# Row maxima of eight heads in one VectorE instruction over two PSUM banks

## The chip, the cores and the metric

The kernel runs on one core of a Trainium2 chip. The metric is device time in microseconds of one execution. The chip's engines, each with its own instruction queue: PE (TensorE, the matrix engine), VectorE (DVE in the rows), ScalarE (ACT), GpSimd (POOL) and SyncE (SP). They meet only at semaphores. PE writes its results to PSUM, which has eight banks of 512 float32 columns on 128 partitions; VectorE and ScalarE read them there.

## The reference

The input is x, 16 sequences of 128 tokens with 128 features. A first layer is a transformer block with conditioning: normalisation, attention with 16 heads of 8 features (q and k normalised and rotated), projection, then a gated feed-forward. A second layer is a linear attention. The change touches the softmax of the first layer only:

```python
attn = jnp.einsum('bnhd,bmhd->bhnm', q, k) * scale
attn = jax.nn.softmax(attn, axis=-1)
o = jnp.einsum('bhnm,bmhd->bnhd', attn, v).reshape(B, N, C)
```

For each sequence and each head this needs the maximum over 128 keys for each of 128 queries, so that the exponential is taken of scores less their maximum.

## The kernel before

All work is scheduled by hand. Each engine has a function `step(t, p)` that holds its share of several sequences at different stages; `steps` runs it for t from −5 to 16. Steps 3 to 10 are a hardware loop with two steps a pass, the others are written out. In step t the scores and their row maxima belong to sequence t + 1, the softmax and the values to sequence t, the splitting of q and k into bf16 parts ("cut", L1282 to L1291) to sequence t + 2, the square sums of q and k ("seed", L1301 to L1311) to sequence t + 4, and the output to sequence t − 1. Within an engine the order is that of the code; `wait` and `wait_ge` hold an engine until a semaphore has reached a value.

The scores of a sequence are made twice. The first time PE writes them as q·k into two banks in turn, `S_BANK` = (0, 1), four heads (512 columns) a bank, in four chunks: `scores(0)` to `scores(3)` (L1468). VectorE takes the row maxima of each chunk with `rowmax(c)` (L1268), negated, into `nmax`. When all 16 are there, VectorE casts them to bf16 in two parts (L1358, L1363), PE transposes them (L1507), and in the next step `weighted(c)` (L1453, L1454) computes scores less maxima in the banks 2 and 3, from which ScalarE takes the exponential (L1062) into `probs`. `values` (L1480) multiplies by v.

`stack(half)` (L1498) is eight PE transposes of q and k parts into bank 4. `stack(0)` serves sequence t + 2, and VectorE copies it to `qT` and `kT` (L1348 to L1350); `stack(1)` is the other half, copied by ScalarE.

What orders the work around the row maxima:
- `scores(c)` overwrites the bank that `rowmax(c − 2)` has read, so it waits for that maximum (`s_max`, raised once by each `rowmax`).
- `rowmax(c)` waits for `scores(c)` (`s_s`).
- In a step PE's order is stack(1), scores(0), transposes (L1507, L1512, L1517), weighted(0), weighted(1), scores(1), L1526, L1530, weighted(2), scores(2), stack(0), projection (L1537), weighted(3), scores(3), values, L1547.
- VectorE's order is cut(0), the padding of v (L1319), L1325, cut(1), L1331, rowmax(0), cut(2), rowmax(1), rowmax(2), the copies of the stack bank, rowmax(3), seed(0) (L1301), the cast L1358, seed(1) (L1305), L1363, L1367, seed(2) (L1307), seed(3) (L1311), L1374.
- GpSimd takes the result of seed(3) through a Newton iteration (L998 to L1004), scales the rotated q and k (L1007), and prepares the next sequence (L965 to L993).

After the attention the same banks 0 and 1 serve the feed-forward (`GU_BANK`), whose first matmul waits for the last row maximum.

Of the kernel before, what the change touches and what calls it, by code (L numbers as in the profile page):

```python
# [26 lines left out]
F32 = mybir.dt.float32  # L27
# [5 lines left out]
B, T, D = 16, 128, 128  # L33
# [14 lines left out]
HPC = 4  # L48
NC = H // HPC
# [23 lines left out]
def is_seq(b):  # L73

    return not isinstance(b, int) or 0 <= b < B


def wait(eng, sem, value):

    if not isinstance(value, int) or value > 0:  # L80
        eng.wait_ge(sem, value)
# [44 lines left out]
def dit_then_linear_attention(nc, x, cond, pos, norm1_w, qkv_w, q_norm_w, k_norm_w, proj_w, proj_b,  # L126
                              norm2_w, w1, w3, w2, ada_w, ada_b, norm_g, norm_b, Wq, bq, Wk, bk, Wv,
                              bv, emb_W, emb_b, sn_g, sn_b, out_W, out_b, out):
    ctx = ExitStack()
    with ctx:  # L130
# [76 lines left out]
        nmax = [sb(f"nmax{p}", [128, H]) for p in range(2)]  # L207
# [44 lines left out]
        hg = two("hg", UNIT, T)  # L252
        res = sb("res", [128, B, D])

        bank = [ctx.enter_context(nc.psum_tensor(f"bank{i}", [128, 512], F32)) for i in range(8)]
        S_BANK, E_BANK, STACK_BANK, P_BANK, O_BANK, W_BANK = (0, 1), (2, 3), 4, 5, 6, 7
        GU_BANK, F_BANK, FT_BANK, X_BANK = (0, 1, 4), 2, 3, 7

# [34 lines left out]
        s_s = sem("s_s")  # L293
        s_max = sem("s_max")
# [476 lines left out]
        def blocks_tensor(e, start=None):  # L771
            q = nc.tensor
# [6 lines left out]
            def b_step(t, p):  # L779
                def hidden(c):  # L780
                    u = t + 1
                    if is_unit(u):
                        if c == 0:
                            e.wait_ge(b_hT, u + 1)
                            if at(u, 0):
                                e.wait_ge(s_max, NC * B)
                                e.wait_ge(s_st1, B)
                        wait(e, b_ff, FC * (u - 1) + c + 1)
                        q.matmul(bank[GU_BANK[c]][:, 0:UNIT * T], w1T[:, c * 128:c * 128 + 128], flat(hT2[1 - p]), start=True, stop=True)  # L789
                        q.matmul(bank[GU_BANK[c]][:, UNIT * T:], w3T[:, c * 128:c * 128 + 128], flat(hT2[1 - p]), start=True,  # L790
                                 stop=True).then_inc(b_gu, 1)

                def back(c):
                    if is_unit(t):
                        e.wait_ge(b_ff, FC * t + c + 1)
                        if c == 0:
                            wait(e, b_fg, t)
                            if at(t, 0):
                                e.wait_ge(s_p, NC * B)
                        last = q.matmul(bank[F_BANK][:, 0:UNIT * T], w2T[:, c, :], ff[c][:, :], start=c == 0, stop=c == FC - 1)  # L800
                        if c == FC - 1:
                            last.then_inc(b_fm, 1)
                back(0)
                hidden(0)
                if is_unit(t + 2):
                    e.wait_ge(b_xs, t + 3)
                    wait(e, b_hT, t + 2)
                    turned(bank[X_BANK], lambda j: xs2[p][:, j, :], b_xsT)
                back(1)
                back(2)  # L810
                hidden(1)
                hidden(2)
                if is_unit(t):
                    e.wait_ge(b_fg, t + 1)
                    wait(e, b_x2, t)
                    turned(bank[FT_BANK], lambda j: fg[:, j, :], b_fgT)
# [340 lines left out]
        def _(v):  # L1157
            q = nc.vector
# [101 lines left out]
            def step(t, p):  # L1260
                q0, q1 = p, (p + 1) % 2
                def rowmax(c):
                    if is_seq(t + 1):
                        b = t + 1
                        v.wait_ge(s_s, NC * b + c + 1)
                        if c == 0:
                            wait(v, s_mp, b - 1)
                        q.tensor_reduce(nmax[q1][:, c * HPC:(c + 1) * HPC],  # L1268
                                        bank[S_BANK[c % 2]][:, :].rearrange("p (h t) -> p h t", t=T),
                                        X_AXIS, ALU.max, negate=True).then_inc(s_max, 1)  # L1270


                def cut(k):
                    b = t + 2
                    if not is_seq(b):
                        return
                    both = parts[q0][:, :, :, :].rearrange("p s h (k d) -> p (s h) k d", d=DH)
                    pq = parts[q0][:, 0, :, :].rearrange("p h (k d) -> p h k d", d=DH)
                    pk = parts[q0][:, 1, :, :].rearrange("p h (k d) -> p h k d", d=DH)
                    if k == 0:  # L1280
                        v.wait_ge(s_hi, b + 1)
                        q.tensor_tensor(rest[:, :, :], rot[q0][:, :, :], both[:, :, 2, :], ALU.subtract).then_inc(s_parts, 1)  # L1282
                    if k == 1:
                        v.wait_ge(s_parts, PARTS * b + 1)
                        q.tensor_copy(both[:, :, 5, :], rest[:, :, :]).then_inc(s_parts, 1)
                    if k == 2:
                        v.wait_ge(s_parts, PARTS * b + 2)
                        q.tensor_tensor(pq[:, :, 4, :], rest[:, 0:H, :], pq[:, :, 5, :], ALU.subtract).then_inc(s_parts, 1)
                        q.tensor_tensor(pk[:, :, 1, :], rest[:, H:, :], pk[:, :, 5, :], ALU.subtract).then_inc(s_parts, 1)
                        q.tensor_copy(pq[:, :, 3, :], pq[:, :, 5, :]).then_inc(s_parts, 1)  # L1290
                        q.tensor_copy(pk[:, :, 0, :], pk[:, :, 5, :]).then_inc(s_parts, 1)  # L1291


                def seed(k):
                    b = t + 4
                    if not is_seq(b):
                        return
                    if k == 0:
                        v.wait_ge(s_sq, b + 1)
                        wait(v, s_newton, NEWT * (b - 2) + NEWT)  # L1300
                        q.tensor_reduce(qv_ms[q0][:, :], qk2[q0][:, :, :], X_AXIS, ALU.add).then_inc(s_ss, 1)  # L1301
                    else:
                        v.wait_ge(s_ss, SEED * b + k)
                    if k == 1:
                        q.tensor_scalar(qv_s[q0][:, :], qv_ms[q0][:, :], 0.5 / DH, 0.5 * EPS0, ALU.mult, ALU.add).then_inc(s_ss, 1)  # L1305
                    if k == 2:
                        q.tensor_scalar(qv_ms[q0][:, :].bitcast(I32), qv_s[q0][:, :].bitcast(I32), 1, None,  # L1307
                                        ALU.logical_shift_right).then_inc(s_ss, 1)
                    if k == 3:
                        wait(v, s_rot, ROT * (b - 2) + ROT)  # L1310
                        q.tensor_scalar(qv_y[q0][:, :].bitcast(I32), qv_ms[q0][:, :].bitcast(I32), -1.0,  # L1311
                                        float(MAGIC - 2 ** 22), ALU.mult, ALU.add).then_inc(s_ss, 1)

                cut(0)
                if is_seq(t):
                    b = t
# [16 lines left out]
                if is_seq(t + 5) and before(t, POOL_NORMS):  # L1333
                    b = t + 5
                    wait(v, s_xsT, b - 1)
                    q.tensor_scalar(xs[q1][:, :], xin[:, bass.ds(b, 1), :].rearrange("p a f -> p (a f)"),  # L1336
                                    rstd_x[:, bass.ds(b, 1)], None, ALU.mult).then_inc(s_xs, 1)
                rowmax(0)
                cut(2)
                rowmax(1)  # L1340
                rowmax(2)
                if is_seq(t + 2):
                    b = t + 2
                    v.wait_ge(s_st, 2 * b + 1)
# [3 lines left out]
                    q.tensor_copy(qT[q0][:, js, :], sb_[:, 0, :, :])  # L1348
                    q.tensor_copy(kT[q0][0:64, js, 0, :], sb_[0:64, 1, :, :])
                    q.tensor_copy(kT[q0][64:128, js, 1, :], sb_[64:128, 1, :, :]).then_inc(s_st0, 1)  # L1350
                rowmax(3)
                seed(0)
                if is_seq(t + 1):

                    b = t + 1
                    v.wait_ge(s_max, NC * b + NC)
                    wait(v, s_mTp, b)
                    q.tensor_copy(mparts[:, 0:H], nmax[q1][:, :]).then_inc(s_mh, 1)  # L1358
                seed(1)
# [30 lines left out]
        def _(e):  # L1390
# [50 lines left out]
            def step(t, p):  # L1441
# [15 lines left out]
                def scores(c):  # L1457
                    if not is_seq(t + 1):
                        return
                    b = t + 1  # L1460
                    if c == 0:
                        e.wait_ge(s_st0, b + 1)
                    if c == NC // 2:
                        e.wait_ge(s_st1, b + 1)
                    wait(e, s_max, NC * b + c - 1)
                    for i in range(HPC // 2):
                        j = c * (HPC // 2) + i
                        last = q.matmul(bank[S_BANK[c % 2]][:, i * 2 * T:(i + 1) * 2 * T], qT[q1][:, j, :],  # L1468
                                        kT[q1][:, j, :, :].rearrange("p s t -> p (s t)"), start=True, stop=True)
                    last.then_inc(s_s, 1)  # L1470
# [118 lines left out]
```

## Time and profile before

| | |
|---|---|
| median of 3 runs | 277.7 us (276.43 to 277.9) |
| profiled execution, span from first to last instruction | 274.4 us |
| time of the profiled execution around its span | not on the page |
| PE busy | 214.6 us (78%) |
| VectorE busy | 220.0 us (80%) |
| ScalarE busy | 169.7 us (62%) |
| GpSimd busy | 158.6 us (58%) |
| row maxima (L1268) | 64 instructions, 42.6 us |

The shares are averages over the loading of weights (to about 40 us), the attention steps (to about 165 us) and the feed-forward and second layer. A row of the timeline has start and duration in us from the span's start; PE's records overlap since matmuls are pipelined. In brackets stands the idle time of the engine before the row and what ended it.

### The profile page before, as it was taken

How to read it: one execution, taken by the hardware profiler on the slowest of the kernel's cores; microseconds unless marked ns; L12 is line 12 of the kernel's file. 1: busy time of each engine (PE TensorE's matmuls, PEld its weight loads, DVE VectorE, ACT ScalarE, POOL GpSimd, SP SyncE). 2: the span in 40 equal slices, each digit the busy share in tenths (PEclk: the TensorE clock that was granted, in tenths of full speed). 3: DMA queues.
4: the chain of work that ended last, by engine and by line, in shares of the span. 5: the costliest groups of instructions: out<-in, count | busy, mean ns of one | idle time of the engine just before them, and what ended most of it. 6: DMA issues, size and time to landing. Idle time of an engine off the chain costs nothing. (4 is left out here: it accounts for less than half of the span.)

```text
span 274.4 us, 7061 instructions
## 1 busy us (share of the span) xinstructions
PE 214.6 (78%) x2028; PEld 162.0 (59%) x2028; DVE 220.0 (80%) x700; ACT 169.7 (62%) x437; POOL 158.6 (58%) x431
## 2 busy tenths in 40 slices
PE   3406196998999989889899999599994899756763
PEld 2403053777677767767677777488882588533531
DVE  7495979899999999999999962587888899946322
ACT  0526235789898989889898875324340377654661
POOL 6184778888888887778887500011207486785300
PEclk9999565699999999999999999979999799995555
DMA  7710000000000000000000000000000000000112
GB/s 147 207 36 0 2 0 0 4 2 0 4 4 4 0 0 0 0 0 0 0 4 0 2 2 1 1 4 0 0 0 0 0 4 1 2 0 0 39 38 76
DMA packets 9554, 4.01 MB, mean 15 GB/s; under 512 B 2669, under 2 KB 9530, under 8 KB 9530
## 3 DMA queue, kind: packets, MB, share of 16 engines
q1 hardware_dynamic: 4170, 2.18, 2.9%
q10 hardware_dynamic: 5360, 1.54, 2.4%
q8 instruction: 11, 0.18, 0.3%
q14 instruction: 13, 0.11, 0.1%
HBM read 2.67 MB, written 1.05 MB: 14 GB/s over the span
## 5 line engine op out<-in xcount | busy, mean ns | idle before, releaser
L1268 DVE TENSOR_REDUCE nmax<-bank 128x4 f32<-128x512 f32 x64 | 42.6, 682 | 2.5 <-PE bank L1468 2.0
L1062 ACT ACTIVATE probs<-bank 128x512 f32<-128x512 f32 x64 | 37.6, 603 | 4.4 <-PE bank L1454 4.3
L1453 PE MATMUL bank<-qT,kT 128*128 128x128 bf16 x256 | 34.6, 222 | 0.3
L1454 PE MATMUL bank<-mT,sel 128*128 128x128 bf16 x256 | 34.5, 222 | 0.0
L1453 PEld LDWEIGHTS bank<-qT,kT 128*128 128x128 bf16 x256 | 25.4, 100 | 4.0 <-ACT mT L1095 1.3
L1454 PEld LDWEIGHTS bank<-mT,sel 128*128 128x128 bf16 x256 | 25.5, 99 | 2.8 <-issue 2.5
L1468 PE MATMUL bank<-kT,qT 128*128 128x256 bf16 x128 | 25.4, 282 | 0.6 <-DVE nmax L1268 0.6
L430 POOL TENSOR_TENSOR xs<-x,rstd 128x256 f32<-128x256 f32 x8 | 4.8, 612 | 32.6 <-DVE rstd L396 19.0
L543 ACT ACTIVATE th<-bank 128x256 f32<-128x256 f32 x24 | 9.2, 384 | 21.0 <-PE bank L776 11.1
L1498 PE MATMUL bank<-identb,parts 128*128 128x128 bf16 x256 | 20.8, 228 | 1.5 <-DVE kT L1350 0.9
L1498 PEld LDWEIGHTS bank<-identb,parts 128*128 128x128 bf16 x256 | 17.5, 104 | 5.2 <-DVE parts L1291 2.5
L1088 ACT ACTIVATE parts<-rot 128x384 bf16<-128x384 f32 x32 | 16.4, 523 | 6.5 <-POOL rot L1007 6.4
L1530 PE MATMUL bank<-qkvT,hT 128*128 128x384 f32 x32 | 16.0, 588 | 4.0 <-ACT hT L1102 4.0
L1480 PE MATMUL bank<-probs,vpad 128*32 128x128 f32 x512 | 17.7, 277 | 0.0
L1512 PE MATMUL bank<-ident,xs 128*128 128x128 f32 x16 | 5.3, 332 | 15.7 <-DVE xs L1336 15.7
L998 POOL TENSOR_TENSOR qv_t<-qv_y 128x32 f32<-128x32 f32 x48 | 12.2, 254 | 7.7 <-DVE qv_y L1311 4.5
L1002 POOL TENSOR_TENSOR qv_t<-three_halves,qv_t 128x32 f32<-128x32 f32 x48 | 14.3, 299 | 3.8
L1000 POOL TENSOR_TENSOR qv_t<-qv_t,qv_s 128x32 f32<-128x32 f32 x48 | 14.2, 297 | 3.8
L876 PE MATMUL bank<-hs,outw 128*128 128x256 f32 x16 | 9.6, 705 | 7.5 <-DVE hs L764 7.5
L1480 PEld LDWEIGHTS bank<-probs,vpad 128*32 128x32 f32 x512 | 12.6, 109 | 4.2 <-issue 3.2
L776 PE MATMUL bank<-ident,xs 128*128 128x128 f32 x48 | 11.4, 327 | 4.5 <-POOL xs L430 4.5
L789 PE MATMUL bank<-hT,w1T 128*128 128x256 f32 x48 | 14.7, 390 | 0.0
(247 smaller groups left out, 683.0 us busy)
## 6 DMA issues: line engine op xcount, KB each, us to landing
out_dram<-res SPq DMA_DIRECT2D x4, 256.0 KB, 2.3
xin<-in_x_dram ACTq DMA_DIRECT2D x1, 768.0 KB, 8.3
ada_n<-in_L_cond_ada_w_dram ACTq DMA_DIRECT2D x1, 384.0 KB, 3.7
xin<-in_x_dram ACTq DMA_DIRECT2D x1, 256.0 KB, 4.1
w_n<-in_L_cond_w_dram SPq DMA_DIRECT2D x2, 128.0 KB
qkv_n<-in_L_cond_qkv_w_dram SPq DMA_DIRECT2D x1, 192.0 KB, 4.5
w_n<-in_L_cond_w_dram SPq DMA_DIRECT2D x1, 170.5 KB
emb_n<-in_L_cond_emb_W_dram SPq DMA_DIRECT2D x1, 128.0 KB
```

What stands on the lines that cost most here:

```text
L789: q.matmul(bank[GU_BANK[c]][:, 0:UNIT * T], w1T[:, c * 128:c * 128 + 128], flat(hT2[1 - p]), start=True, stop=True)
L1000: q.tensor_tensor(t_, t_, s_, ALU.mult).then_inc(s_newton, 1)
L1002: q.tensor_tensor(t_, three_halves[:, :], t_, ALU.subtract).then_inc(s_newton, 1)
L1062: q.activation(probs[c][:, :, :].rearrange("p h t -> p (h t)"), bank[E_BANK[c % 2]][:, :], ACT.Exp, scale=SCALE).then_inc(s_p, 1)
L1088: last = q.activation(slots, rot[q1][:, s * H:(s + 1) * H, :].unsqueeze(2).to_broadcast([128, H, 3, DH]), ACT.Copy)
L1268: q.tensor_reduce(nmax[q1][:, c * HPC:(c + 1) * HPC], bank[S_BANK[c % 2]][:, :].rearrange("p (h t) -> p h t", t=T), X_AXIS, ALU.max, negat ...
L1453: q.matmul(dst, kT[q0][:, h // 2, h % 2, :], qT[q0][:, h // 2, :], start=True, stop=False)
L1454: last = q.matmul(dst, sel[:, h, :], mT[q0][:, :], start=False, stop=True)
L1468: last = q.matmul(bank[S_BANK[c % 2]][:, i * 2 * T:(i + 1) * 2 * T], qT[q1][:, j, :], kT[q1][:, j, :, :].rearrange("p s t -> p (s t)"), st ...
L1480: last = q.matmul(bank[O_BANK][VW * i:VW * (i + 1), c * T:(c + 1) * T], vpad[q0][:, c * HPC + i, :], probs[c][:, i, :], start=True, stop=True)
L1498: last = q.transpose(bank[STACK_BANK][:, at:at + T // 2].bitcast(BF16), src[:, s, h:h + 2, :].rearrange("p h k -> p (h k)"), identb[:, :])
L1530: q.matmul(bank[W_BANK][:, 0:3 * D], hT[q0][:, :], qkvT[:, :], start=True, stop=True).then_inc(s_qkv, 1)
```

## The change

Banks 0 and 1 become one PSUM tensor of 1024 columns, `both_s`. `rowmax(c)` is called twice instead of four times and reads both banks: rowmax(0) the eight heads of scores(0) and scores(1), rowmax(1) those of scores(2) and scores(3). The semaphore `s_max` rises by two a sequence instead of four, and the waits follow: scores(0) and scores(1) wait for both maxima of the sequence before, scores(2) and scores(3) for rowmax(0) of their own. On VectorE cut(2) now stands ahead of rowmax(0), and seed(0) ahead of rowmax(1).

```diff
-        bank = [ctx.enter_context(nc.psum_tensor(f"bank{i}", [128, 512], F32)) for i in range(8)]
+        both_s = ctx.enter_context(nc.psum_tensor("both_s", [128, 1024], F32))
+        bank = [both_s[:, 0:512], both_s[:, 512:1024]]
+        bank += [ctx.enter_context(nc.psum_tensor(f"bank{i}", [128, 512], F32)) for i in range(2, 8)]
@@ feed-forward, first unit
-                                e.wait_ge(s_max, NC * B)
+                                e.wait_ge(s_max, 2 * B)
@@ rowmax(c)
-                        v.wait_ge(s_s, NC * b + c + 1)
+                        v.wait_ge(s_s, NC * b + 2 * c + 2)
                         if c == 0:
                             wait(v, s_mp, b - 1)
-                        q.tensor_reduce(nmax[q1][:, c * HPC:(c + 1) * HPC],
-                                        bank[S_BANK[c % 2]][:, :].rearrange("p (h t) -> p h t", t=T),
+                        q.tensor_reduce(nmax[q1][:, c * 2 * HPC:(c + 1) * 2 * HPC],
+                                        both_s[:, :].rearrange("p (h t) -> p h t", t=T),
                                         X_AXIS, ALU.max, negate=True).then_inc(s_max, 1)
@@ VectorE, step
+                cut(2)
                 rowmax(0)
-                cut(2)
-                rowmax(1)
-                rowmax(2)
                 if is_seq(t + 2):
...
-                rowmax(3)
                 seed(0)
+                rowmax(1)
                 if is_seq(t + 1):
 
                     b = t + 1
-                    v.wait_ge(s_max, NC * b + NC)
+                    v.wait_ge(s_max, 2 * b + 2)
@@ PE, scores(c)
-                    wait(e, s_max, NC * b + c - 1)
+                    wait(e, s_max, 2 * b + c // 2)
```

VectorE's queue before, in step 2, from the output scaling (L1331) to the square sums (L1301); `s_s` is raised by scores, `s_st` by stack, `s_e` by weighted:

```order
L1331 TENSOR_TENSOR o<-bank,rsum 128x128 [waits s_oTp,s_rec]
L1268 TENSOR_REDUCE nmax<-bank 128x4 [waits s_mp,s_s]
L1288 TENSOR_TENSOR parts<-rest,parts 128x16x8 [waits s_parts]
L1289 TENSOR_TENSOR parts<-rest,parts 128x16x8
L1290 COPY parts<-parts 128x16x8
L1291 COPY parts<-parts 128x16x8
L1268 TENSOR_REDUCE nmax<-bank 128x4 [waits s_s] x2
L1348 COPY qT<-bank 128x512 [waits s_e,s_st]
L1349 COPY kT<-bank 64x4x128
L1350 COPY kT<-bank 64x4x128
L1268 TENSOR_REDUCE nmax<-bank 128x4 [waits s_s]
L1301 TENSOR_REDUCE qv_ms<-qk 128x32 [waits s_newton,s_sq]
```

The same piece of VectorE's queue now (lines are two further on in parts of the file: L1290 to L1293 is the cut, L1270 the row maximum, L1303 the square sums):

```order
L1333 TENSOR_TENSOR o<-bank,rsum 128x128 [waits s_oTp,s_rec]
L1290 TENSOR_TENSOR parts<-rest,parts 128x16x8 [waits s_parts]
L1291 TENSOR_TENSOR parts<-rest,parts 128x16x8
L1292 COPY parts<-parts 128x16x8
L1293 COPY parts<-parts 128x16x8
L1270 TENSOR_REDUCE nmax<-both_s 128x8 [waits s_mp,s_s]
L1348 COPY qT<-bank 128x512 [waits s_e,s_st]
L1349 COPY kT<-bank 64x4x128
L1350 COPY kT<-bank 64x4x128
L1303 TENSOR_REDUCE qv_ms<-qk 128x32 [waits s_newton,s_sq]
L1270 TENSOR_REDUCE nmax<-both_s 128x8 [waits s_s]
L1358 CAST mparts<-nmax 128x16 [waits s_mTp,s_max]
```

The cut moved ahead of the first row maximum, one row maximum of 128x8 stands where three of 128x4 stood, directly ahead of the copy L1348, and the last one went behind the square sums. PE's queue has the same order as before; only the values it waits for are others.

## Rows read from the trace of the kernel before

**Rows 1.** Windows, attention: length; busy PE, PEld, DVE, ACT, POOL; clock; DMA share; GB/s.

```profile
60.00:140.00 80.00, 72.97 (x1050) 57.34 (x1051) 78.03 (x246) 71.90 (x178) 66.33 (x187) 1.00 0.00 1
```

**Rows 2.** Page, part 2: tenths in 40 slices of 6.9 us, PE and clock.

```profile
PE   3406196998999989889899999599994899756763
...
PEclk9999565699999999999999999979999799995555
```

**Rows 3.** Timeline of VectorE, one step: start, duration, line, operation, out<-in, count.

```profile
119.02 0.18 DVE L1311 TENSOR_SCALAR qv_y<-qv_ms 128x32 int32<-128x32 int32 x1
...
119.89 0.28 DVE L1319 TENSOR_SCALAR vpad<-vall 128x128 f32 x1
...
120.66 0.68 DVE L1268 TENSOR_REDUCE nmax<-bank 128x4 f32<-128x512 f32 x1
121.26 0.28 DVE L1288 TENSOR_TENSOR parts<-rest,parts 128x128 bf16<-128x128 f32 x1
...
121.98 1.27 DVE L1268 TENSOR_REDUCE nmax<-bank 128x4 f32<-128x512 f32 x2
123.18 0.41 DVE L1348 COPY qT<-bank 128x512 bf16<-128x512 bf16 x1
...
124.39 0.69 DVE L1268 TENSOR_REDUCE nmax<-bank 128x4 f32<-128x512 f32 x1
125.00 0.41 DVE L1301 TENSOR_REDUCE qv_ms<-qk 128x32 f32<-128x256 f32 x1
125.32 0.19 DVE L1358 CAST mparts<-nmax 128x16 bf16<-128x16 f32 x1
125.44 0.49 DVE L1305 TENSOR_SCALAR qv_s<-qv_ms 128x32 f32<-128x32 f32 x1
...
126.52 0.51 DVE L1311 TENSOR_SCALAR qv_y<-qv_ms 128x32 int32<-128x32 int32 x1
...
127.15 0.48 DVE L1282 TENSOR_TENSOR rest<-rot,parts 128x256 f32<-128x256 f32 x1
```

**Rows 4.** Timeline of VectorE: L1319 of two sequences, ten steps apart.

```profile
65.42 0.27 DVE L1319 TENSOR_SCALAR vpad<-vall 128x128 f32<-128x128 f32 x1
...
142.87 0.26 DVE L1319 TENSOR_SCALAR vpad<-vall 128x128 f32<-128x128 f32 x1
```

**Rows 5.** Timeline of PE in the same step: scores(2) and stack(0).

```profile
122.13 0.38 PE L1468 MATMUL bank<-kT,qT 128*128 128x256 bf16 x2
122.35 0.61 PE L1498 MATMUL bank<-identb,parts 128*128 128x128 bf16 x8
```

**Rows 6.** Timeline of PE and VectorE at half clock: handovers between them.

```profile
36.73 1.03 PE L1498 MATMUL bank<-identb,parts 128*128 128x128 bf16 x8
...
37.80 0.42 DVE L1348 COPY qT<-bank 128x512 bf16<-128x512 bf16 x1 [1.13 <-PE bank L1498]
...
43.27 0.68 DVE L1268 TENSOR_REDUCE nmax<-bank 128x4 f32<-128x512 f32 x1
...
44.10 0.59 PE L1468 MATMUL bank<-kT,qT 128*128 128x256 bf16 x2 [0.56 <-DVE nmax L1268]
```

**Rows 7.** Groups by line and shape: out<-in, count | busy us, mean ns | idle before.

```profile
L1268 DVE TENSOR_REDUCE nmax<-bank 128x4 f32<-128x512 f32 x64 | 42.6, 682 | 2.5 <-PE bank L1468 2.0
...
L736 DVE TENSOR_REDUCE kmax<-bank 128x2 f32<-128x256 f32 x8 | 3.3, 414 | 0.0
```

**Rows 8.** Timeline of GpSimd: start of two Newton stretches, and L993.

```profile
119.29 0.24 POOL L998 TENSOR_TENSOR qv_t<-qv_y 128x32 f32<-128x32 f32 x1 [0.43 <-DVE qv_y L1311]
...
126.42 0.57 POOL L993 TENSOR_TENSOR rot<-rot,partner 128x192 f32<-128x192 f32 x1
127.11 0.24 POOL L998 TENSOR_TENSOR qv_t<-qv_y 128x32 f32<-128x32 f32 x1
```

**Rows 9.** Timeline of VectorE in step 14.

```profile
158.82 0.69 DVE L1268 TENSOR_REDUCE nmax<-bank 128x4 f32<-128x512 f32 x1 [0.47 <-PE bank L1468]
```


## The prediction

> **What bounds the kernel now.** I read the busy digits of the page first, then the windows over the attention steps, then VectorE's timeline through one step, and last PE and GpSimd beside it. From 60 to 140 us VectorE is busy 78.03 of 80.00 us, PE 72.97, ScalarE 71.90 and GpSimd 66.33, at full clock [rows 1, 2]. So in this stretch VectorE is the bound, and a wait that it gains is paid in full unless something of its own shrinks. One step (one sequence through the pipeline) lasts (142.87 − 65.42) / 10 = 7.75 us [rows 4]. There are 15 steps in which VectorE does both row maxima and the copy out of the stack bank (t = −1 to 13), and one more, t = 14, with row maxima alone.
>
> The order to see in one step [rows 3]: row maximum 0 at 120.66, the cut of q and k in four instructions from 121.26, row maxima 1 and 2 from 121.98, the copies of the stack bank (L1348 to L1350) from 123.18, row maximum 3 at 124.39, the square sums (L1301) at 125.00. Meanwhile PE makes scores(2) at 122.13 and the eight transposes of stack(0) at 122.35, which end at 122.96 [rows 5]. The copies begin 0.22 us after that. PE's work for the copies is thus hidden under row maxima 1 and 2; VectorE doesn't wait for it.
>
> **What the change saves.** A row maximum over 512 columns takes 682 ns, and the same kind of instruction over 256 columns, also from PSUM, takes 414 ns [rows 7]: 268 ns for 256 columns. Over 1024 columns that gives 682 + 536 = 1218 ns. Back to back, row maxima start 0.60 us apart (120.66 to 121.26; the pair of 1.27 us less 0.68 [rows 3]), so one merged instruction saves 0.60 − 0.54 = 0.06 us. Two per step, 16 steps: 2.0 us. That is all that the merge can give. No row shows one instruction that reads two banks; bounds are 1.07 us (nothing but a pace of 268 ns for 256 columns) and 1.36 us (twice 682 ns). I take 1.22.
>
> The Trainium skill ("Perfetto Trace Analysis", Optimizing Scalar/DVE Operations) gives about 125 ns of access overhead for each VectorE instruction on PSUM; by that the 32 instructions that go would be worth 4.0 us, where the rows say 2.0. [...]
>
> **What the change adds.** PE's order is unchanged: weighted(2), scores(2), stack(0), projection, weighted(3), scores(3), values. But scores(2) overwrites bank 0, and now it waits for the merged row maximum 0, which reads both banks. VectorE's next instruction behind that maximum is the copy of the stack bank, which needs stack(0), which stands behind scores(2) on PE. So the link row maximum → scores(2) → stack(0) → copy lies bare, every step. Queued behind the copy are the square sums, row maximum 1 and everything else of VectorE. Price of the link:
> - end of the row maximum to the start of scores: 43.27 + 0.68 = 43.95 to 44.10, 0.15 us [rows 6]
> - scores(2) to the first transpose: 122.35 − 122.13 = 0.22 us [rows 5]
> - eight transposes: 0.61 us [rows 5]
> - end of the transposes to the copy: 36.73 + 1.03 = 37.76 to 37.80, 0.04 us [rows 6]
>
> Sum 1.02 us; with the half clock of the first steps the transposes are 1.03 and the scores 0.59 [rows 6], so about 1.6.
>
> Now one step as offsets from its start (L1319 at 119.89 = 0). Cut(2) takes the place of row maximum 0 at 0.77 and lasts 0.72; row maximum 0 runs from 1.49 to 2.71; the copy starts at 3.73 (before: 3.29). The copies hold VectorE 1.21 (123.18 to 124.39), so the square sums start at 4.94, row maximum 1 runs from 5.26 to 6.48, the cast of the maxima follows at 6.52, and L1305 starts at 6.64 instead of 5.55 [rows 3]. That is +1.09 us. The saving of the merge is inside this number: both merged maxima are now followed by an instruction that waits for their end, so the usual overlap of 0.08 us is gone as well.
>
> The other new waits are not last. Row maximum 0 wants scores(1), which PE has finished before cut(2) is through. Scores(0) of the next step wants row maximum 1, but the transpose of the maxima, next on PE, wants the cast and the difference after it, which come later anyway.
>
> **What comes back.** The small instructions L1305 to L1311 are slowed by GpSimd: L1311 at 126.52 takes 0.51 us and ends at 127.03, just as GpSimd's L993 ends at 126.99; at 119.02, with GpSimd idle, it takes 0.18 [rows 3, 8]. The Trainium skill ("SBUF — State Buffer", Two separate sides) calls the port pair that the two share an exclusive lock for a whole instruction; the trace agrees with the 0.33 us above. GpSimd needs 126.99 − 119.29 = 7.70 us from the start of one Newton stretch to the end of L993 [rows 8], nearly the whole step of 7.75. If the step grows by more than half a microsecond, GpSimd falls silent for that time right before the next Newton stretch, where L1307 and L1311 lie. That gives back at least the 0.33 us of L1311, at most about 0.9 (if L1305, L1363 and L1307 are held too, as 0.49 for L1305 suggests). L1305 at offset 6.64 still meets L993, so I take 0.4. Net: 1.09 − 0.40 = +0.69 us a step.
>
> **The sum.** Steps 1 to 11: 11 × 0.69 = 7.6. Steps 12 and 13 have no square sums and no Newton work on GpSimd, so nothing comes back: 2 × 1.09 = 2.2. Steps −1 and 0 lie at about half clock, with a link of about 1.6, but VectorE had some slack there; I estimate 1.2 each, 2.4. Step 14 has no copy and VectorE already waited for PE (0.47 us [rows 9]); scores(2) comes about 0.6 later. Together 12.8 us. What follows (the feed-forward and the second layer) starts when attention lets it and is moved as a whole. Span 274.4 + 12.8 = 287.2; the median of the runs, 277.7, is 3.3 above the profiled span, which I keep: 290.5, rounded to **290 us**. The page gives no time around its span, so 3.3 is that difference alone.
>
> **Rivals.**
> 1. *Nothing comes back from GpSimd.* Its instructions keep meeting VectorE's because everything moves together. Then 13 × 1.09 + 2.4 + 0.6 = 17.2: 295 us. For it: steps of different length all show such holds. Against: at 7.70 us of work GpSimd can't fill a step of 8.8.
> 2. *Everything comes back.* With GpSimd silent the whole stretch L1305 to L1311 runs free, 0.9 less; a step costs 1.09 − 0.9 = 0.2, so 11 × 0.2 + 2.2 + 2.4 + 0.6 = 7.4: 285 us. Shorter handovers (0.05 for 0.15) could make it 283.
> 3. *The wait stays hidden, the merge pays.* Deciding point: scores(2) and stack(0) would have to be done while the maximum is still running, that is the link below about 0.1 us a step, or the relief above 1.1 on each. Then the 2.0 us of saved starts remain: 275.7 us, not slower. Against it stands PE's order, and that scores(2) may not touch bank 0 earlier. The change would have to not do what it says.
> 4. *The clock.* PE idles more: 72.97 of 80 us is 91%, which is 7.06 us a step; in a step of 8.4 us that is 84%. The digits show a clock of 5 to 7 tenths only around slices in which PE was busy 1 to 6 tenths, and 9 where it was 8 [rows 2]. If a few slices still fell to half clock, the link grows by 0.6 us there and the 7.06 us of PE work stops fitting: some 10 us more, 300 us.
>
> **Chances.** Forecast 0.54 (its own range 286 to 294), rival 1 0.2, rival 2 0.15, rival 3 0.04, rival 4 0.07. The range for 8 in 10 reaches over rivals 1 and 2 as far as 283.5 and 296.5. The measurement of this kernel can tell about 0.5% (1.4 us) from no change. Slower 0.94, same 0.03 and faster 0.03 (rival 3 split between them, with a little of rival 2).
>
> **What would show it.** In the profile after: VectorE's reduce 128x8 at 1.22 us, 32 of them; idle time before L1348 put down to PE's transposes, about 1.0 us, 15 times; PE idle before scores(2), put down to the row maximum; VectorE's busy share in the attention stretch down from 97% to about 87%; steps of about 8.4 us; and L1313 (L1311 before) near 0.18 us instead of 0.5. The forecast is wrong if L1348 is not waited for, if the reduce takes more than 1.36 us, or if GpSimd's holds are the same. A time below 280 would mean that VectorE was not the bound of the step.

## The result and the profile after

The changed kernel takes 287.19 us (median of 4 runs, 286.05 to 288.37) against 277.51 us (276.43 to 277.9) before. The ratio is 1.0351, 95% interval 1.0309 to 1.0393: 9.7 us slower. The forecast was 290 us. Some executions of a kernel fall over 1.5% behind its fastest; ratios leave them out, while medians and ranges hold all runs.

The page of the changed kernel, span and digits (these answer to [rows 2]):

```profile
span 285.8 us, 7021 instructions
...
PE   3407296988888888898887889969998689954773
...
PEclk9999999799999999999999999969999599996555
```

The window over the attention steps (answers to [rows 1]): in the same 80 us VectorE is busy 67.66 us instead of 78.03, and PE 69.26 instead of 72.97, at full clock. No engine is busy for more than 87% of the stretch any more (the forecast had said that of VectorE, which shows 85%); the engines wait for each other.

```profile
60.00:140.00 80.00, 69.26 (x945) 52.22 (x942) 67.66 (x207) 66.57 (x163) 61.85 (x173) 1.00 0.00 1
```

The groups of the merged row maximum, of PE's scores and of the copy, with the idle time before them on their engine:

```profile
L1270 DVE TENSOR_REDUCE nmax<-both_s 128x8 f32<-128x1024 f32 x32 | 39.0, 1218 | 3.5 <-PE both_s L1468 3.0
...
L1468 PE MATMUL both_s<-kT,qT 128*128 128x256 bf16 x128 | 25.8, 285 | 12.6 <-DVE nmax L1270 12.4
...
L1348 DVE COPY qT<-bank 128x512 bf16<-128x512 bf16 x16 | 6.8, 424 | 17.0 <-PE bank L1498 17.0
```

One merged maximum takes 1218 ns. The copy L1348, for which VectorE had waited once in 16 times, is now waited for 16 times out of 16, 17.0 us in all (15 of them new, as forecast), and each time it is PE's transposes (L1498) that end the wait. PE in turn waits 12.4 us for the row maxima.

VectorE through one step (answers to [rows 3]; L1321 was L1319, L1290 was L1288, L1270 was L1268, L1303 was L1301, L1307 was L1305, L1313 was L1311):

```profile
118.83 0.27 DVE L1321 TENSOR_SCALAR vpad<-vall 128x128 f32 x1
...
119.53 0.28 DVE L1290 TENSOR_TENSOR parts<-rest,parts 128x128 bf16<-128x128 f32 x1
...
120.24 1.21 DVE L1270 TENSOR_REDUCE nmax<-both_s 128x8 f32<-128x1024 f32 x1
122.38 0.42 DVE L1348 COPY qT<-bank 128x512 bf16<-128x512 bf16 x1 [0.94 <-PE bank L1498]
...
123.60 0.42 DVE L1303 TENSOR_REDUCE qv_ms<-qk 128x32 f32<-128x256 f32 x1
124.05 1.22 DVE L1270 TENSOR_REDUCE nmax<-both_s 128x8 f32<-128x1024 f32 x1
125.31 0.17 DVE L1358 CAST mparts<-nmax 128x16 bf16<-128x16 f32 x1
125.42 0.53 DVE L1307 TENSOR_SCALAR qv_s<-qv_ms 128x32 f32<-128x32 f32 x1
...
126.45 0.18 DVE L1313 TENSOR_SCALAR qv_y<-qv_ms 128x32 int32<-128x32 int32 x1
```

PE and GpSimd in the same step (answers to [rows 5] and [rows 8]):

```profile
119.47 0.38 PE L1468 MATMUL both_s<-kT,qT 128*128 128x256 bf16 x2
...
121.50 0.39 PE L1468 MATMUL both_s<-kT,qT 128*128 128x256 bf16 x2 [0.42 <-DVE nmax L1270]
121.73 0.61 PE L1498 MATMUL bank<-identb,parts 128*128 128x128 bf16 x8
...
125.33 0.39 PE L1468 MATMUL both_s<-kT,qT 128*128 128x256 bf16 x2 [0.15 <-DVE nmax L1270]
126.16 0.23 PE L1507 MATMUL bank<-identb,mparts 128*128 128x128 bf16 x1 [0.44 <-DVE mparts L1363]
```

```profile
118.39 0.24 POOL L1000 TENSOR_TENSOR qv_t<-qv_y 128x32 f32<-128x32 f32 x1 [0.99 <-DVE qv_y L1313]
...
125.32 0.59 POOL L995 TENSOR_TENSOR rot<-rot,partner 128x192 f32<-128x192 f32 x1
126.71 0.24 POOL L1000 TENSOR_TENSOR qv_t<-qv_y 128x32 f32<-128x32 f32 x1 [0.80 <-DVE qv_y L1313]
```

The row maximum ends at 121.45. PE starts scores(2) at 121.50 and the transposes at 121.73, which end at 122.34, and VectorE goes on at 122.38 after 0.94 us of nothing. L1313 takes 0.18 us, as L1311 did when GpSimd was idle, and GpSimd now waits 0.80 and 0.99 us for it. Ten steps (answers to [rows 4]) last 84.41 us, 8.44 each instead of 7.75:

```profile
67.76 0.26 DVE L1321 TENSOR_SCALAR vpad<-vall 128x128 f32<-128x128 f32 x1
...
152.17 0.26 DVE L1321 TENSOR_SCALAR vpad<-vall 128x128 f32<-128x128 f32 x1
```

### The profile page after: what moved, and what is told of

The parts are those of the page before. It is cut to its first block and busy times, and to the rows that moved or that the text cites. A ratio compares the mean times of both kernels' runs of the same rounds, so it can differ in the third digit from the quotient of the medians.

```text
span 285.8 us, 7021 instructions
## 1 busy us (share of the span) xinstructions
PE 221.2 (77%) x2028; PEld 164.6 (58%) x2028; DVE 213.2 (75%) x668; ACT 169.9 (59%) x437; POOL 159.4 (56%) x431
## 5 line engine op out<-in xcount | busy, mean ns | idle before, releaser
L1270 DVE TENSOR_REDUCE nmax<-both_s 128x8 f32<-128x1024 f32 x32 | 39.0, 1218 | 3.5 <-PE both_s L1468 3.0
L1468 PE MATMUL both_s<-kT,qT 128*128 128x256 bf16 x128 | 25.8, 285 | 12.6 <-DVE nmax L1270 12.4
L1000 POOL TENSOR_TENSOR qv_t<-qv_y 128x32 f32<-128x32 f32 x48 | 13.0, 270 | 16.6 <-DVE qv_y L1313 14.1
L1498 PE MATMUL bank<-identb,parts 128*128 128x128 bf16 x256 | 20.8, 228 | 1.0 <-DVE kT L1350 0.9
L1498 PEld LDWEIGHTS bank<-identb,parts 128*128 128x128 bf16 x256 | 17.6, 104 | 4.2 <-issue 2.2
L1468 PEld LDWEIGHTS both_s<-kT,qT 128*128 128x128 bf16 x128 | 9.3, 101 | 18.2 <-DVE nmax L1270 8.1
L1530 PE MATMUL bank<-qkvT,hT 128*128 128x384 f32 x32 | 17.0, 620 | 3.3 <-ACT hT L1104 3.3
L1348 DVE COPY qT<-bank 128x512 bf16<-128x512 bf16 x16 | 6.8, 424 | 17.0 <-PE bank L1498 17.0
L1512 PE MATMUL bank<-ident,xs 128*128 128x128 f32 x16 | 5.5, 341 | 14.9 <-DVE xs L1338 14.9
L545 ACT ACTIVATE th<-both_s 128x256 f32<-128x256 f32 x16 | 6.1, 384 | 18.2 <-PE bank L778 11.9
L1006 POOL TENSOR_TENSOR qv_y<-qv_y,qv_t 128x32 f32<-128x32 f32 x48 | 13.1, 274 | 3.8
L802 PE MATMUL bank<-ff,w2T 128*128 128x256 f32 x48 | 14.5, 414 | 0.7 <-DVE ff L675 0.7
```

The lines of the kernel that those rows point to most:

```text
L1270: q.tensor_reduce(nmax[q1][:, c * 2 * HPC:(c + 1) * 2 * HPC], both_s[:, :].rearrange("p (h t) -> p h t", t=T), X_AXIS, ALU.max, negate=Tru ...
L1498: last = q.transpose(bank[STACK_BANK][:, at:at + T // 2].bitcast(BF16), src[:, s, h:h + 2, :].rearrange("p h k -> p (h k)"), identb[:, :])
L1530: q.matmul(bank[W_BANK][:, 0:3 * D], hT[q0][:, :], qkvT[:, :], start=True, stop=True).then_inc(s_qkv, 1)
```

## The experiments

Two theories were put against each other. **A**: the bare link row maximum, scores(2), stack(0), copy costs about 1.0 us a step, and GpSimd gives about 0.4 back, because it no longer holds VectorE's small instructions. **B**: what costs is that the second maximum is complete later, and with it all that follows it. "Step" is the mean of the ten steps from the padding of v of sequence 2 to that of sequence 12, in the one profiled run of each kernel. Ratios are against the kernel before on the same chip. Spans of single profiles differ by 1 us and more through the stretches before and behind the attention, so small differences in time are read from the ratios.

**e1: stack(0) ahead of scores(2) on PE.**

```diff
                 weighted(2)
-                scores(2)
                 stack(0)
+                scores(2)
```

> The changed kernel, but on PE stack(0) is issued ahead of scores(2), so that the copies of the stack bank no longer stand behind the merged row maximum. Theory A (the bare link row maximum, scores(2), stack(0), copy costs about 1.0 us a step, GpSimd gives 0.4 back): the idle time before L1348 (1.0 us, 16 times in the changed kernel) is gone, GpSimd's holds return, steps go from 8.44 back to about 7.7 to 7.8 us, and the kernel takes 276 to 279 us, near the one before. Theory B (what costs is the late second maximum: the maxima of a sequence reach PE later and the softmax of the next step with them): scores(2) and the second maximum come no earlier than now, so 285 to 289 us, with PE idle before the transposes of the maxima as in the changed kernel.

Measured 278.51 us, ratio 1.004 (1.0013 to 1.0067). VectorE and PE in one step:

```profile
122.80 0.28 DVE L1321 TENSOR_SCALAR vpad<-vall 128x128 f32 x1
...
124.29 1.21 DVE L1270 TENSOR_REDUCE nmax<-both_s 128x8 f32<-128x1024 f32 x1
125.79 0.42 DVE L1348 COPY qT<-bank 128x512 bf16<-128x512 bf16 x1 [0.29 <-PE bank L1498]
...
128.72 0.18 DVE L1358 CAST mparts<-nmax 128x16 bf16<-128x16 f32 x1
```

```profile
123.79 0.32 PE L1526 MATMUL bank<-ident,o 128*128 128x128 f32 x1 [0.42 <-DVE o L1333]
...
125.05 0.61 PE L1498 MATMUL bank<-identb,parts 128*128 128x128 bf16 x8
125.56 0.39 PE L1468 MATMUL both_s<-kT,qT 128*128 128x256 bf16 x2
```

Of the 9.7 us all but about 1 are gone, by the order of two groups on PE; the merge is still there. So the link is what cost most of it, and theory B as it stood is out. The attention itself gives back less than the whole kernel. The last padding of v starts at 165.41 us before, at 176.66 in the changed kernel and at 169.27 here, so 3.9 of 11.3 us are left there. What follows it takes 106.8 us here and 109.0 before, and in the last 28 us of the span the mean granted clock was 0.56 here and 0.51 before. Whether that stretch is shorter in every run of e1 is not shown. The step is 7.97 us, though, not the 7.7 to 7.8 expected, and the copy still waits 0.29 us: PE reaches stack(0) at 125.05 only, since L1526 has waited for VectorE's L1333 and the projection of q, k and v and weighted(2) come after it. PE has an earliest time for these transposes that does not come from the maxima of this step.

**e2: the change without the merge.** Four row maxima in pairs, each over its own bank again; scores(2) waits for both of the first pair. The cuts show the waits and the order alone.

```diff
-                        v.wait_ge(s_s, NC * b + 2 * c + 2)
+                        v.wait_ge(s_s, NC * b + c // 2 * 2 + 2)
...
                 rowmax(0)
+                rowmax(1)
...
                 seed(0)
-                rowmax(1)
+                rowmax(2)
+                rowmax(3)
...
-                    wait(e, s_max, 2 * b + c // 2)
+                    wait(e, s_max, NC * b + c // 2 * 2)
```

> The changed kernel's order and waits, but four row maxima of four heads (128x512), in two pairs: scores(2) waits for both maxima of the first pair. This is the change without the merge. Theory A: the link is as bare as in the changed kernel; each pair takes 0.60 + 0.68 = 1.28 us instead of 1.22, so 32 x 0.06 = 2 us more than the changed kernel: about 289 us. If the read over two banks had a cost of its own, this kernel would be the faster one, below 286 us.

Measured 289.95 us, ratio 1.0433 (1.0398 to 1.0468): 2.8 us above the changed kernel by the medians, 2.3 by the ratios. The merge saves what the rows promised, 2 us or a little more, and the reading over two banks shows no cost: 1218 ns, where 682 ns and the measured pace had given 1218. The order and the waits lose 12.2 us.

**e3: as e2, but with the finer waits of the kernel before** (`rowmax(c)` waits for scores(c), scores(c) for rowmax(c − 2)).

```diff
-                        v.wait_ge(s_s, NC * b + c // 2 * 2 + 2)
+                        v.wait_ge(s_s, NC * b + c + 1)
...
-                    wait(e, s_max, NC * b + c // 2 * 2)
+                    wait(e, s_max, NC * b + c - 1)
```

> Four row maxima again in the order of the changed kernel (cut(2), maxima 0 and 1, copies, square sums, maxima 2 and 3), but with the finer waits of the kernel before: scores(2) waits for maximum 0 only. Theory A: the link starts 0.6 us earlier, so the copy waits 0.4 us instead of 1.0; the step is then about 0.4 to 0.5 us longer than before, less what GpSimd gives back (0.2 or so): 280 to 283 us. Theory B: the second pair is as late as in the changed kernel: 287 us or more.

Measured 282.26 us, ratio 1.0162 (1.0132 to 1.0192). VectorE waits 4.9 us in 12 steps before the copy, 0.4 each, as expected. The finer waits (scores(2) on maximum 0 alone instead of on both, and likewise for the other chunks) are worth 7.7 us.

**e4: cut(2) behind row maximum 0**, in the changed kernel.

```diff
-                cut(2)
                 rowmax(0)
+                cut(2)
```

> The changed kernel with cut(2) behind the merged row maximum 0, as in the kernel before. Theory A: scores(2) runs on PE while VectorE cuts (0.72 us), and what lies bare is only the end of the cut to the copy: 0.1 + 0.61 + 0.04 = 0.75 us instead of 1.0. Steps 0.2 to 0.25 us shorter than 8.44, 283 to 285 us. Theory B: the second maximum comes 0.25 us earlier as well, the same time, so this run does not tell the two apart by itself, but its wait before L1348 should be 0.75 us.

Measured 287.58 us, ratio 1.0361 (1.0321 to 1.04): no gain, a miss. The wait before L1348 is 0.72 us as computed, but another has come:

```profile
120.87 1.23 DVE L1270 TENSOR_REDUCE nmax<-both_s 128x8 f32<-128x1024 f32 x1 [0.28 <-PE both_s L1468]
...
123.46 0.42 DVE L1348 COPY qT<-bank 128x512 bf16<-128x512 bf16 x1 [0.72 <-PE bank L1498]
```

Row maximum 0 needs scores(1) now at a time when PE has just made them: 0.28 us of idle time. PE cannot make them earlier, since they stand behind weighted(0) and weighted(1), which need the maxima of the sequence before. In the changed kernel scores(1) ended at 119.85, and the maximum began at 120.24 with the cut ahead of it: this second limit lies only 0.4 us behind the first. So the copy starts no earlier in its step: 3.65 us after the padding of v at 119.81, against 3.55.

**e5: one part alone, maxima 2 and 3 merged.** Maxima 0 and 1 stay apart in their old places.

```diff
-                cut(2)
                 rowmax(0)
+                cut(2)
+                rowmax(1)
...
                 seed(0)
-                rowmax(1)
+                rowmax(2)
...
-                    wait(e, s_max, 2 * b + c // 2)
+                    wait(e, s_max, 3 * b + max(c - 1, 0))
```

> One part of the change alone: row maxima 0 and 1 stay apart and in their old places, only maxima 2 and 3 become one instruction over both banks, behind the copies and the square sums. Scores(2) waits for maximum 0 only. Theory A: between maximum 0 and the copies VectorE still has the cut (0.72 us) and maximum 1 (0.60 us), which is more than the link of 1.0 us, so nothing waits before L1348; the merge gives 0.06 us a step and loses the overlap with the cast, 0.08: 277 to 279 us, no difference to the kernel before. Theory B (the late second maximum costs): the maxima of a sequence are complete 0.5 to 0.6 us later after the copies than before, as in the changed kernel, so most of the loss should be here: 283 us or more.

Measured 280.05 us, ratio 1.0105 (1.0081 to 1.0129): above the range of A. VectorE and PE in one step:

```profile
123.26 0.27 DVE L1321 TENSOR_SCALAR vpad<-vall 128x128 f32 x1
...
125.36 0.68 DVE L1270 TENSOR_REDUCE nmax<-both_s 128x4 f32<-128x512 f32 x1
126.46 0.42 DVE L1349 COPY qT<-bank 128x512 bf16<-128x512 bf16 x1 [0.43 <-PE bank L1499]
...
128.13 1.23 DVE L1270 TENSOR_REDUCE nmax<-both_s 128x8 f32<-128x1024 f32 x1
129.39 0.35 DVE L1359 CAST mparts<-nmax 128x16 bf16<-128x16 f32 x1
```

```profile
124.24 0.33 PE L1527 MATMUL bank<-ident,o 128*128 128x128 f32 x1 [0.23 <-DVE o L1333]
...
125.50 0.38 PE L1469 MATMUL both_s<-kT,qT 128*128 128x256 bf16 x2
125.72 0.61 PE L1499 MATMUL bank<-identb,parts 128*128 128x128 bf16 x8
```

Theory A had compared the link with VectorE's work behind maximum 0. But PE starts scores(2) at 125.50, 0.79 us after maximum 0 (124.03 to 124.71) has ended; it is late for its own reasons, as in e1. The copy starts 3.20 us after the start of the step (123.26), hardly earlier than before (3.29, [rows 3]). In the kernel before, VectorE used that time for row maximum 2. Merged with maximum 3, this work stands behind the copies, and the cast of the maxima comes at 6.13 instead of 5.43. That is the part of theory B that is true. This version also has the swap of the square sums that e10 takes alone.

**e6: stack(0) ahead of weighted(2) too.**

```diff
+                stack(0)
                 weighted(2)
                 scores(2)
-                stack(0)
```

> As the run with stack(0) ahead of scores(2), but stack(0) stands ahead of weighted(2) too. In that run PE reached stack(0) too late in many steps (idle 0.3 us before L1348), because weighted(2) stood before it. Theory A: the wait before L1348 vanishes, steps of 7.97 us become 7.7 to 7.8, and the kernel takes 275.5 to 278 us. The rival here: weighted(2) and the third exponential come 0.45 us later, and ScalarE, which is busy 70 of 80 us, hands that on: 279 us or more.

Measured 278.72 us, ratio 1.0027 (0.9989 to 1.0065), from 275.71 to 280.51 in 12 runs. No difference to the kernel before that can be measured, and not told apart from e1; the steps of 7.7 us that theory A wanted are not shown: the profiled run, one of the slowest, has 7.93.

**e7 and e8: two Newton iterations on GpSimd instead of three**, in the kernel before and in the changed one. One iteration is left out, so the norms of q and k are less exact.

```diff
-                for k in range(3):
+                for k in range(2):
```

> The kernel before with two Newton iterations on GpSimd instead of three (one iteration, four GpSimd instructions of about 0.27 us, is left out, so the norms are less exact). GpSimd is quiet for 1.3 us a step more, where the small VectorE instructions L1305 to L1311 lie. Theory A with GpSimd's holds: VectorE loses 0.4 to 0.7 us a step in 11 steps, 270 to 274 us. Rival (VectorE's 0.5 us durations there have nothing to do with GpSimd, and the changed kernel's shorter ones neither): 277 to 278 us, unchanged, since VectorE bounds the step.

> The changed kernel with two Newton iterations on GpSimd instead of three (one iteration is left out, so the norms are less exact). GpSimd is already silent 0.8 to 1.0 us a step; one hold of 0.35 us (L1358 or L1307) is left in a step. Theory A: only that one goes, 0.3 to 0.4 us in 11 steps, 282.5 to 284 us, and the distance to the kernel before with two iterations is larger than the 9.7 us of the full pair: 11 to 14 us, because nothing is given back any more. Rival: 287 us, and a distance of 9.7.

Measured 270.47 us, ratio 0.9754 (0.9729 to 0.9778), for the kernel before, and 283.33 us, ratio 1.0236 (1.0203 to 1.0269), for the changed one: all inside what theory A said, 12.9 us apart instead of 9.7. GpSimd's work lengthens VectorE's step, though VectorE was the busiest engine. VectorE's small instructions in e7, where 0.19, 0.49 and 0.51 us had stood in [rows 3] for L1358, L1305 and L1311:

```profile
113.87 0.54 DVE L1358 CAST mparts<-nmax 128x16 bf16<-128x16 f32 x1
114.33 0.17 DVE L1305 TENSOR_SCALAR qv_s<-qv_ms 128x32 f32<-128x32 f32 x1
...
114.76 0.17 DVE L1307 TENSOR_SCALAR qv_ms<-qv_s 128x32 int32<-128x32 int32 x1
115.07 0.18 DVE L1311 TENSOR_SCALAR qv_y<-qv_ms 128x32 int32<-128x32 int32 x1
```

With less work on GpSimd, the change costs a third more, because less is given back. GpSimd is not wholly out of the way in e7: one hold is left in each step and lies on the cast now (0.54 us instead of 0.17 to 0.19), while in e8 no small instruction is held (all take 0.17 to 0.18). So 12.9 us still holds about 0.36 us a step that GpSimd takes from the kernel before and not from the changed one. It also tells against rival 2 of the prediction: e8 is faster than the changed kernel by 3.2 us by the ratios and 3.9 by the medians, so GpSimd had not given back everything.

**e9: e6 with two Newton iterations.**

```diff
+                stack(0)
                 weighted(2)
                 scores(2)
-                stack(0)
...
-                for k in range(3):
+                for k in range(2):
```

> The changed kernel with stack(0) ahead of weighted(2) on PE and with two Newton iterations on GpSimd instead of three (one is left out). Here neither the link nor GpSimd's holds should be left, so what remains against the kernel before with two iterations (270.5 us) is the merge itself. Theory A: two starts of 0.06 us saved and two overlaps of 0.08 us lost a step, no difference: 269.5 to 271.5 us. Rival (the merged maxima cost something of their own, such as the later second maximum, which showed as steps of 7.93 us against 7.75 in the full kernels): 0.2 us in 11 steps and more, 272.5 to 274 us.

Measured 273.09 us, ratio 0.9834 (0.9802 to 0.9867), against 0.9754 for e7, 2.2 us more by the ratios: in the rival's range. But the waits between 60 and 155 us (engine, line, waited for: us in total, times, longest) name another cause than the merge:

```profile
PE bank L1498 <- ACT kT L1080: 5.6, 12, 0.7
DVE qT L1348 <- PE bank L1498: 3.7, 10, 0.7
```

PE holds stack(0) until ScalarE has copied the other half out of the same bank (L1080), and VectorE waits 3.7 us for stack(0). The expectation had overlooked this limit. These waits are larger than the 2.2 us of difference, so this run says nothing on a price of the merge itself.

**e10: the kernel before with one swap**, square sums ahead of row maximum 3.

```diff
-                rowmax(3)
                 seed(0)
+                rowmax(3)
```

> The kernel before with one swap on VectorE: the square sums stand ahead of row maximum 3 instead of behind it, as in the changed kernel. No merge, no link (scores(2) needs only maximum 0). Theory A with holds: the cast no longer overlaps with anything (0.1 us a step) and the small instructions meet GpSimd at another moment, so that GpSimd ends L993 before the last of them and then waits 0.4 us for it, as in the runs with stack(0) moved: 278.5 to 280 us. Rival: the swap is neutral and the 1 to 3 us left in those runs and in the one with the second pair alone come from the merge: 277 to 278 us.

Measured 278.93 us, ratio 1.0042 (1.0022 to 1.0061), 1.2 us slower (0.8 by the medians): inside theory A's range, near its lower end, though the kernel before was at 278.12 in these runs. The step is (145.81 − 66.64) / 10 = 7.92 us:

```profile
66.64 0.26 DVE L1319 TENSOR_SCALAR vpad<-vall 128x128 f32<-128x128 f32 x1
...
145.81 0.27 DVE L1319 TENSOR_SCALAR vpad<-vall 128x128 f32<-128x128 f32 x1
```

The swap alone, with no merge and no link, makes the step nearly as long as in e1 and e5. It is part of the change; the forecast had 0.08 us a step for it, the overlap that the cast loses, about 1 us in all.

**e11: e6 with the square sums behind row maximum 1 again.**

```diff
+                stack(0)
                 weighted(2)
                 scores(2)
-                stack(0)
...
-                seed(0)
                 rowmax(1)
+                seed(0)
```

> The changed kernel with stack(0) ahead of weighted(2) on PE and the square sums behind row maximum 1 on VectorE, as in the kernel before. Theory A: no wait before L1348, the cast overlaps with the square sums again, the step is 0.1 us shorter than before: 275.5 to 277.5 us, the first version with merged maxima that is not slower than the kernel before. Rival (what is left in the run with stack(0) alone is the price of the merge): 278 to 279.5 us, unchanged.

Measured 277.76 us, ratio 0.9997 (0.9968 to 1.0025): between the two ranges, and like e6 not told apart from the kernel before. VectorE no longer waits before the copy, but it waits for scores(3), 0.3 us a step:

```profile
DVE nmax L1270 <- PE both_s L1468: 4.0, 12, 0.4
```

The step is 7.94 us and the last padding of v comes at 167.75, 2.3 us later than before. In the profiled run the time is equal through what follows it, 106.8 us instead of 109.0, again at a mean granted clock of 0.56 instead of 0.51 in the last 28 us. So no version with both merges is shown to have an attention as fast as that of the kernel before.

## Why the prediction was right, point by point

The steps of five kernels side by side; offsets are from the padding of v in the steps shown above or in [rows 3] (for e7, from its trace at 108.51):

| | copy starts | cast starts | step | time |
|---|---|---|---|---|
| before | 3.29 | 5.43 | 7.75 | 277.5 |
| changed | 3.55 | 6.48 | 8.44 | 287.2 |
| e1, stack(0) first | 2.99 | 5.92 | 7.97 | 278.5 |
| e5, one merge | 3.20 | 6.13 | 7.98 | 280.1 |
| e7, before, GpSimd light | 3.22 | 5.36 | 7.34 | 270.5 |

- **The merge.** Forecast 1.22 us for one maximum and 2.0 us in all; the group shows 1218 ns, and e2 against the changed kernel 2.3 to 2.8 us, nearer to the 2.0 of the rows than to the 4.0 that the prediction also names. Right.
- **The link.** Forecast 1.02 us bare in each step; idle before L1348 is 0.94 to 1.03 us at full clock, and 1.62 and 1.35 in the two steps at the start for which 1.6 was taken. Right, and e1 shows that it is the main cause.
- **The offsets.** Forecast for the copy 3.73 and for L1305 6.64 after the start of the step; measured 3.55 and 6.59, and 3.73 for the copy in the next step. The second maximum starts 0.45 us after the square sums and not 0.32, which makes up for an early copy in one step and makes the cast 0.14 us late in the other. Right.
- **What comes back.** Forecast 0.40 us a step with L1313 free at 0.18; measured L1313 at 0.18, and 7.75 + 1.18 (the mean delay of the cast over the ten steps) − 8.44 = 0.49. Right, with e7 and e8 behind it. That one hold would stay was foreseen too: L1307 takes 0.53 us.
- **The sum.** Forecast 12.8 us of span, measured 285.8 − 274.4 = 11.4. Steps 1 to 11 were forecast at 7.6 and took 9.30 − 1.75 = 7.55 more. Steps −1 and 0 took 1.75 instead of 2.4. Steps 12 and 13 took 1.4 instead of 2.2: the cast came 0.98 and 0.93 us later, not 1.09, and the kernel before had a wait of 0.30 us for GpSimd in the one and a hold longer by 0.12 us in the other. The rest is 0.7 against 0.6.
- **Around the span.** The forecast added 3.3 us, the distance of the median to one span. Every run listed with its span shows 2.0 to 2.2 (287.85 and 285.8; 277.44 and 275.4). By that the profiled run of before, with a span of 274.4, was the one of 276.43, 1.3 us below the median of 277.7, and that of the changed kernel 0.7 above its own, so the distance came out as 1.4. The error of 2.8 us is 1.4 from the sum and 1.9 from this term, less 0.5 of rounding. By the medians the change costs 9.7 us, not the 11.4 of the two spans.
- **Rivals.** Nothing comes back (295), hidden (276), the clock (300): none of them. The granted clock was 1.00 from 60 to 155 us. Everything comes back (285) lies nearer to the measured 287.19 than the forecast does, so the time alone does not decide between them; what rules it out is the one hold of about 0.36 us that is left in a step, and e8, where it is gone. One reading for the clock rival was not exact: of the six slices in which PE was busy 8 tenths, one shows a clock of 7 and not 9 [rows 2].

Where the forecast had a gap that did not show: it spoke of one bound, VectorE's queue, and of idle time there that is paid in full. e4, e5, e9 and e11 each ran into another wait 0.3 to 0.6 us behind: scores(1) behind the previous maxima, PE's own earliest time for stack(0), ScalarE's copy of the bank, scores(3).

The traces show a loop over GpSimd and VectorE as well. In the kernels with three Newton iterations, between 80 and 140 us, GpSimd takes 7.44 to 7.82 us from the start of a Newton stretch to the end of L993 (L995 in the changed kernel). One of VectorE's small instructions always ends 0.02 to 0.05 us behind that. VectorE then does what is left up to L1311 (L1313), for which the next Newton stretch waits. In e10 L993 runs from 129.03 to 129.60 and the next Newton stretch starts at 130.04, and on VectorE stand between them:

```profile
129.10 0.53 DVE L1307 TENSOR_SCALAR qv_ms<-qv_s 128x32 int32<-128x32 int32 x1
...
129.78 0.18 DVE L1311 TENSOR_SCALAR qv_y<-qv_ms 128x32 int32<-128x32 int32 x1
```

So the step is GpSimd's stretch and the rest behind it, and the rest depends on which instruction is held (named as in the kernel before):

| | held at the end of L993 | from there to the next Newton stretch | step |
|---|---|---|---|
| before | L1311 (3 of 7 times) or L1307 (4 of 7) | 0.12 to 0.13 or 0.43 to 0.44 | 7.75 |
| e1, e3, e5, e6, e10, e11 | L1307 (in one step of e6 and of e11 L1311) | 0.42 to 0.45 (0.11 and 0.12) | 7.92 to 8.06 |
| changed, e2, e4 | L1305, L1363 or the cast L1358 | 0.73 to 1.00 | 8.44 to 8.53 |

Six kernels with waits of 0 to 0.46 us before the copy have nearly the same step. In them a wait of VectorE that ends early enough seems to shorten a hold and not to lengthen the step. By this reading the waits that e4, e5 and e11 ran into need not be what set their steps, and the swap of e10 costs because L1307 is held in every step instead of in some. It was read from the traces afterwards, and no run tests it alone. It does not touch the first cause: in e8, where nothing is held, the step is 8.14 us with the link, and in e7 it is 7.34 without it and with one hold.

## What to carry to other kernels

Before joining two instructions, write down who waits for the first of them: the join makes that waiter wait for the second as well, and if the waiter's result is what your own engine needs next, the whole round trip becomes idle time. Here a merge worth 2 to 3 us came with waits and an order that cost 12, and the order of two groups on another engine decided most of it. When several engines are near full, a gain on one is soon a wait for the next, so count the slack of each limit; and a loss may be softened in the same way.

## What was not expected

- GpSimd was busy for 66.33 of 80 us in the attention stretch and VectorE for 78.03, yet four GpSimd instructions less per step (about 1.3 us) made the kernel before 6.7 us faster (e7). The busy time of VectorE contained the time in which GpSimd held it, as the 0.49 and 0.51 us of L1305 and L1311 [rows 3] beside 0.17 and 0.18 in e7 show.
- The digits of the granted clock at the start differ from run to run (5 and 6 tenths between 27 and 55 us in the kernel before, 9 in the changed one up to 50 us), while in the changed kernel the eight transposes at 45.66 us took 1.06 us, as at half clock. At the start of this kernel the durations of PE's instructions say more than the digits.
